# The last three dense graph layers and the norm between them as one stage of 21 blocks

## The reference, cut to what matters

```python
x = x + gated(relu(layernorm(x)))                  # gated layer
x = x + attention(relu(layernorm(x)))              # two attention layers
# from here on: the part that this case is about
h = relu(layernorm(x))
x = x + segment_sum(h[src], dst) / max(deg, 1)     # mean layer
h = relu(layernorm(x))
t = relu(h @ W_self1 + mean_dst(h[src]) @ W_neigh1 + b1)        # first sage layer
x = x + t @ W_self2 + mean_dst(t[src]) @ W_neigh2 + b2          # second sage layer
```

## Time and profile before

| | |
|---|---|
| median of 3 runs | 2992.27 us (2991.39 to 2993.29) |
| the profiled execution | 2988.12 us, its span 2986.0 us |
| from the first matmul of the first dense layer to the end of the span | 2605.6 to 2986.0 us |
| PE busy over the span | 2342.4 us (78%) |
| DVE, ACT, POOL busy over the span | 2250.7, 1007.8, 862.4 us |
| mean granted clock of PE over the span | 0.915 of full speed |

### The profile page before, as it was taken

The page is one execution under the profiler, slowest core; times in us unless marked ns, Lnnn a source line. Parts: engine busy times, 40 slices in busy tenths (PEclk is TensorE's granted clock), DMA queues, the critical chain, the costliest instruction groups (busy, mean ns, idle before and its releaser), DMA issues. The chain is left out here.

```text
span 2986.0 us, 52389 instructions
## 1 busy us (share of the span) xinstructions
PE 2342.4 (78%) x12594; PEld 1568.4 (53%) x12708; DVE 2250.7 (75%) x10890; ACT 1007.8 (34%) x2354; POOL 862.4 (29%) x906
## 2 busy tenths in 40 slices
PE   3676597489999999278867899999964888397868
PEld 1444486245555555156663455555532766275656
DVE  5666666889999999954478899999997444745434
ACT  1777696150100000123365100000011335364434
POOL 0000000017777776100000677777730000000101
PEclk8999799699999999599988999999987999697979
DMA  1000600249999999065532899999943554240121
GB/s 27 1 2 3 289 14 6 67 143 340 339 339 330 330 329 321 0 156 162 156 73 97 272 343 335 326 334 329 332 140 77 164 162 111 69 214 27 35 70 29
DMA packets 403361, 514.58 MB, mean 172 GB/s; under 512 B 31435, under 2 KB 337350, under 8 KB 401542
## 3 DMA queue, kind: packets, MB, share of 16 engines
q1 hardware_dynamic: 335266, 235.04, 27.1%
q0 software_dynamic: 66560, 274.39, 25.4%
q10 hardware_dynamic: 1252, 1.80, 0.2%
HBM read 412.46 MB, written 98.65 MB: 171 GB/s over the span
## 5 line engine op out<-in xcount | busy, mean ns | idle before, releaser
L961 POOL DMA_INDIRECT rows<-row_table,idx x832 | 793.4, 954 | 579.8 <-POOLq L140 302.3
L1012 PE MATMUL z_ps<-xr,hot_ta 128*128 x2400 | 660.5, 382 | 50.0 <-DVE rows L1055 19.4
L1023 PE MATMUL z_ps<-rows,ident 128*128 128x256 f32 x1664 | 567.9, 423 | 7.7 <-DMA rows<-row_table,idx 6.5
L1055 DVE SCALAR_TENSOR_TENSOR rows<-rows,att_all 128x128 f32<-128x128 f32 x1664 | 417.2, 287 | 3.5
L1012 PEld LDWEIGHTS z_ps<-xr,hot_ta 128*128 128x128 bf16 x2496 | 241.2, 97 | 326.0 <-issue 211.2
L1055 DVE SCALAR_TENSOR_TENSOR rows<-z_ps,att_all 128x128 f32<-128x128 f32 x1664 | 406.9, 280 | 0.0
L1398 PE MATMUL acc_m<-xr,hot_m 128*128 x1984 | 341.4, 293 | 76.6 <-issue 52.7
L1398 PEld LDWEIGHTS acc_m<-xr,hot_m 128*128 128x128 f32 x1984 | 282.8, 195 | 141.7 <-issue 136.6
L1081 DVE TENSOR_TENSOR rows<-z_ps,rows 128x256 f32<-128x256 f32 x832 | 346.9, 417 | 8.3 <-PE z_ps L1023 8.3
L1023 PEld LDWEIGHTS z_ps<-rows,ident 128*128 128x128 f32 x1664 | 252.6, 192 | 109.6 <-DMA rows<-row_table,idx 14.8
L2249 PE MATMUL dense_ps<-cnt,h_part 128*128 128x512 f32 (+1 forms) x525 | 218.3, 416 | 106.3 <-ACT cnt L2230 93.5
(11 more groups left out here) (442 smaller groups left out, 3652.0 us busy)
## 6 DMA issues: line engine op xcount, KB each, us to landing
xr<-kept_rows SPq DMA_DIRECT2D x124, 512.0 KB, 4.1
kept_rows<-rows SPq DMA_DIRECT2D x416, 128.0 KB, 5.4
spread_a<-rel_rows SPq DMA_DIRECT2D x208, 128.0 KB, 5.3
counts_line<-counts SPq DMA_DIRECT2D x1, 19550.0 KB
counts<-counts_line SPq DMA_DIRECT2D x6, 3200.0 KB, 18.1
rows<-row_table,idx POOLq DMA_INDIRECT x832, 5.7
row_table<-xl_ring SPq DMA_DIRECT2D x50, 258.0 KB, 2.0
rows<-row_table SPq DMA_DIRECT2D x32, 320.0 KB, 7.6
```

Of the source, the lines that this page charges most:

```text
L961: nc.gpsimd.indirect_dma_start(out=rows[:, u, :], out_offset=None, in_=table, in_offset=bass.IndirectOffsetOnAxis(ap=c.idx[:, n:n + 1], ax ...
L1012: nc.tensor.matmul(ps[:, n % Z, :], hot, tile[:, m, 0:HC], start=m == 0, stop=False, skip_group_check=True)
L1023: nc.tensor.matmul(ps[:, n % Z, HALF_C:HC], c.ident[:, :], rows[:, n % ROWS, HALF_C:HC], start=False, stop=True, skip_group_check=True).th ...
L1055: return nc.vector.scalar_tensor_tensor(out=rows[:, n % ROWS, h * C:(h + 1) * C], in0=z, scalar=0.0, in1=g.att[:, h * C:(h + 1) * C], op0= ...
```

## The change

`dense_layer` and its three calls, the second `norm_relu` and the stage of reloads go. One function, `last_layers`, does all three layers in one stage without a barrier inside: 21 blocks g = 0 to 20, seven in each layer, in the order first big, small, then the other five big ones.

- **Small block.** The counts (56 + 8 + 16 = 80 columns) are the weights, and both parts of h, side by side (256 columns), the moving operand: one matmul in a step, no transposing of the sums afterwards. It took two matmuls of 72 columns.
- **Fix.** A big block's fix follows its own last step (for the first two blocks of a layer, step 8 of the third). The one-hot operand is made by DVE, from uint16 numbers.
- **Results in pieces.** `finish` of a block comes after step 4 of the next, and DVE's element work is cut into five or six pieces, placed at steps 7, 10, 11, 14, 19, 20. PSUM sums have 3 banks.
- **Norm inside.** In layer 0 a block's result goes on at once to its layer norm: statistics on DVE, square root, relu and the high part on ACT, the low part on DVE, all tile by tile at the steps of the next block.
- **Reload.** The new parts of h are stored as they are made, and loaded back group by group (5, 4, 4, 4, 4 tiles) in the layer's last block as soon as its matmuls have used the old ones; the last block's own four tiles are written straight to `parts`. The source tiles are taken in the order 24, 0, 1, ..., 23. DVE casts for odd steps and the last one (13), ACT for 12.
- **Counts.** Their 7 transfers are issued in the `norm_relu` before, and nobody waits for them there. `counts` has one window more; `gated_layer` therefore saves one more window, and its ring is `RINGS = 2`.
- x, h and their space: h stays allocated, its space holds `cnt` and `sum_t`; x is stored to `x_line` block by block, its space then holds weights and results.
- At the very end one more clearing of semaphores and one more barrier.

```diff
@@ norm_relu
-                    sp.wait_ge(s["loads"], 16 * loads(sp, s["loads"]))
+                    if (count := loads(sp, s["loads"])) > 0:
+                        sp.wait_ge(s["loads"], 16 * count)
@@ gated_layer
-        RINGS = 3
+        RINGS = 2
-        high_w = counts[:, SPARE:SPARE + PEAK_WINDOWS, :]
+        high_w = counts[:, SPARE:SPARE + 1 + PEAK_WINDOWS, :]
@@ last_layers (for dense_layer)
+    ORDER = [0, SMALL] + list(range(1, SMALL))
+    BUFS = 4
+    SUMS = 3
+    FIX = 8
+    TILES = [NODE_TILES - 1] + list(range(NODE_TILES - 1))
+    GROUPS = [range(0, T + 1)] + [range(j, j + T) for j in range(T + 1, NODE_TILES - T, T)]
...
+                def add(g, j):
...
+                    if layer(g) > 0 and place(g) == 0:
+                        for b, group in enumerate(GROUPS):
+                            if j == group[0]:
+                                pe.wait_ge(s["loaded"][b], layer(g) * 16 * (4 if b == 0 else 2))
+                        if j == GROUPS[-1][-1] + 1:
+                            pe.wait_ge(s["made"], g)
+                    if small(g):
+                        last = nc.tensor.matmul(
+                            sums(g, 0, 2 * P, slice(0, NARROW)).rearrange("p (k c) -> p k c", k=2),
+                            cnt[:, n % BUFS, 0:NARROW], parts[:, :, k, :], start=j == 0, stop=False,
+                            skip_group_check=True)
+                    else:
+                        last = both(sums(g, 0, BANK), [parts[:, b, k, :] for b in range(2)], cnt[:, n % BUFS, :],
+                                    j == 0, False)
...
+                for g in range(CHUNKS):
+                    for j in range(NODE_TILES):
+                        add(g, j)
+                        if place(g) == 2:
+                            if j == FIX:
+                                fix(g - 2)
+                                fix(g - 1)
+                                if layer(g) > 0:
+                                    turn(g - 2)
+                            if j == 13:
+                                finish(g - 2)
+                            if j == 15 and layer(g) > 0:
+                                turn(g - 1)
+                                turn_own(g - 1)
+                            if j == 22 and layer(g) > 0:
+                                finish(g - 1)
+                        if j == 4 and g > 0 and place(g - 1) in BIG:
+                            finish(g - 1)
+                        if j == 23 and place(g) in BIG and layer(g) > 0:
+                            turn(g)
+                    if place(g) in BIG:
+                        fix(g)
+                finish(CHUNKS - 1)
@@ ACT: after the cast of step j
+                        if g > 0 and place(g - 1) in BIG:
+                            if j == 2:
+                                copy_sums(g - 1)
+                                if layer(g - 1) > 0:
+                                    copy_turned(g - 1)
+                            if layer(g - 1) == 0:
+                                if j == 12:
+                                    normalize(g - 1, 0)      # square root, waits for DVE's piece 2
+                                if j == 15:
+                                    normalize(g - 1, 1)      # relu of two tiles, waits for piece 3
+                                if j == 16:
+                                    normalize(g - 1, 2)      # relu of two tiles
+                                if j == 18:
+                                    normalize(g - 1, 3)      # high part of four tiles
...
@@ DVE: after the cast of step j
+                        if place(g) == 2:
+                            if j == 3:
+                                peak_parts(g - 1)
+                            if j == FIX:
+                                peak_hot(g - 2)
+                                peak_hot(g - 1)
+                            if j == 13 and layer(g) > 0:
+                                own_sum(g - 1)
+                            if layer(g) == 0 and j in (16, 17, 18, 21, 24):
+                                result(g - 2, (16, 17, 18, 21, 24).index(j))
+                            if layer(g) > 0 and j in (16, 17, 18, 20, 22, 24):
+                                result(g - 2, (16, 17, 18, 20, 22, 24).index(j))
+                        if place(g) == 3:
+                            if layer(g) == 0 and j in (1, 3, 4, 6, 9):
+                                result(g - 2, (1, 3, 4, 6, 9).index(j))
+                            if layer(g) > 0 and j < 6:
+                                result(g - 2, j)
+                        if g > 0 and place(g - 1) in BIG:
+                            if j in (7, 10, 11, 14, 19):
+                                result(g - 1, (7, 10, 11, 14, 19).index(j))
+                            if j == 20 and layer(g - 1) > 0:
+                                result(g - 1, 5)
+                    if place(g) in BIG:
+                        peak_hot(g)
@@ SP
+                for n in range(LAYERS_ALL - 1):
+                    first, last = n * PER, n * PER + LAST
+                    for g in range(first, last - 1):
+                        if n == 0:
+                            keep_x(g)
+                        keep_parts(g)
+                    load_parts(last, 0)
+                    if n == 0:
+                        keep_x(last - 1)
+                    for b in range(1, len(GROUPS) - 1):
+                        load_parts(last, b)
+                    keep_parts(last - 1)
+                    load_parts(last, len(GROUPS) - 1)
...
@@ graph_layers
-        dense_layer(nc, c, counts, parts, inv_deg, x, dst, counts_line=counts_line)
...
+        def restore(sp, sem):
+            for k, q in enumerate([0, len(chunks) - 1] + list(range(1, len(chunks) - 1))):
+                low, size = chunks[q]
+                size += 1 + PEAK_WINDOWS if q == len(chunks) - 1 else 0
+                sp.dma_start(counts[:, low:low + size, :], counts_line[:, low:low + size, :]).then_inc(restored[k], 16)
+            return 0
+
+        norm_relu(nc, c, x, h, add=h, loads=restore, parts=(parts[:, 0, :, :], parts[:, 1, :, :]))
+        last_layers(nc, c, counts, parts, inv_deg, x, h_wide, dst, restored,
+                    ((W_self1, W_neigh1, b1), (W_self2, W_neigh2, b2)), h_tables, x_line, out)
+        nc.clear_and_free_semaphores(restored)
+        nc.all_engine_barrier()
```

More of the change, by code:

```diff
@@ L2216, in dense_layer @@
-        with phase(nc, cast_a=0, cast_d=0, cast_p=0, used=0, summed=0, sum_t=0, turned=0, h_t=0, prod=0, vec=0, res=0,
-                   nodes=0, numbers=0, nodes_in=0, peaks=0, peak_c=0, high=0, low=0, zeros=0, loads=0, x_in=2, stored=2,
-                   restored=len(chunks)) as (block, s):
-            def cast(engine, copy, o, k, done):
-                n = step(o, k)
-                q, low, size = chunks[o]
-                size = columns_of(o) // W_NODES
-                if k < 2 and counts_line is not None:
-                    engine.wait_ge(s["restored"][o], 16)
+        own_node = sb("peak_node", [PEAK_COLS, PER])
@@ new lines, in last_layers, with _, cast @@
+        with phase(nc, cast_a=0, cast_d=0, hot=0, used=0, summed=0, turned=0, h_t=0, prod=0, vec=0,
+                   left=0, made=0, nodes_in=0, nodes=0, numbers=0, number=0, peak=0, peak_t=0, zeros=0, loads=0,
+                   x_kept=0, kept=0, loaded=len(GROUPS), x_in=2, stored=2, var=0, std=0, scaled=0, normal=0, high=0,
+                   own_part=0, own_sum=0, own_turned=0) as (block, s):
+            @block.gpsimd
+            def _(pool):
+                nc.gpsimd.iota(columns[:, :], [[1, BANK]], base=0, channel_multiplier=0,
+                               allow_small_or_imprecise_dtypes=True).then_inc(s["numbers"], 1)
+            def cast(engine, copy, g, j, done):
+                n, k = step(g, j), TILES[j]
+                low, size = whole[ORDER[place(g)]]
+                if small(g):
+                    size = NARROW // W_NODES
+                if layer(g) == 0 and j < 2:
+                    engine.wait_ge(restored[place(g)], 16)
@@ new lines, in fix @@
+                def fix(g):
+                    n = fix_step(g)
+                    if place(g) == 0:
+                        pe.wait_ge(s["peak_t"], 2 * layer(g) + 2)
+                    pe.wait_ge(s["hot"], g + 1)
+                    hot = cnt[0:PEAK_COLS, n % BUFS, :]
+                    if small(g):
+                        last = nc.tensor.matmul(
+                            sums(g, 0, 2 * P, slice(0, NARROW)).rearrange("p (k c) -> p k c", k=2),
+                            hot[:, 0:NARROW], peak_t[:, :, :], start=False, stop=True, skip_group_check=True)
+                    else:
+                        last = both(sums(g, 0, BANK), [peak_t[:, b, :] for b in range(2)], hot, False, True)
+                    last.then_inc(s["used"], 1)
@@ new lines, in turn, with turn_own @@
+                def turn(g):
+                    if g > PER:
```

(20 more changed lines are left out.)

598 lines of the change are left out of this document (353 added, 245 removed).

## The result

The changed kernel took 2927.11 us (median of 4 runs, 2922.93 to 2931.8) beside 2992.17 us for the kernel before on the same chip: a ratio of 0.9783, 95% interval 0.9766 to 0.98. Its profiled execution took 2922.93 us, with a span of 2921.1 us and a mean clock of 0.925 (forecast: 2910.8 and 2908.7). From the stage's first matmul to the end of the span it is 321.0 us, where it was 380.4.

A forecast was written before the change was run, and what follows sets the result against it. PE's three gaps before the dense layers, 93.5 us, were taken as the bound. Start 2600.6, layers 95.0, 99.1 and 98.4, tail 10.2 and waits 5.4 gave span 2908.7, profiled 2910.8, plus 4.15: 2915 us; range 2898 to 2941.

The forecast's parts named there:

- Start: Stage's first matmul: counts issued 20 us earlier, so PE starts at 2600.6, 5.0 us earlier; transfers cost the norm nothing.
- Block 0: First wide block of the stage: six steps at half clock, then 19 steps by 0.467, 14.0 us.
- Small block: Block with 80 weight columns and 256 moving: a buffer's round trip sets the pace, 4.2 us; bounds 2.7 and 10.7.
- that rival: Clock falls at the small block: it takes 5.3 us and the next 5 us run at half; 2929 us, chance 10%.
- Sage blocks: Big blocks of the sage layers: stall shrinks to some 0.15 us, so 15.4 us each, 15.3 in the last layer.
- the rival in which the pieces don't fit: Big blocks lose 1.5 us each in sage layers, 1 in layer 0: 23 us, 2938 us, chance 13%.
- Layer 0: Big blocks with the norm inside: 14.6 us each; the third 17.0 and the fourth 16.0.
- the 5.4 us added for waits: Allowance of 0.3 us per big block for waits between engines that the walk along PE doesn't see.
- Boundaries: Between layers: both gaps, 42.9 us, go; a reload group, stored and loaded late in the last block, arrives in time.
- The rival of a late reload: A reload group takes 12 us, not 3.5; PE waits about 8 at each boundary: 21 us, 2936 us, chance 9%.
- Clock: PE's clock rises about 5 us after dense work begins; half clock only for the first six steps.
- Tail: From the end of the last fix to the span's end: 10.2 us instead of 10.6, if finish runs at full clock.

The follow-up runs named there:

- e0: The changed kernel run again, unedited, as the control: 2928.62 us.
- e7: Changed kernel, but SP issues the two peak-node loads in the norm, just ahead of the 7 counts transfers: 2903.09 us.
- e1: Changed kernel, but the peak nodes are loaded in the kernel's first phase instead of by SP in the last stage: 2911.41 us.
- e2: Changed kernel, but ACT's queue issues the two peak-node loads at the stage's start instead of SP's: 2907.54 us.
- e6: e2, but in the sage layers a big block's result pieces run in one go behind step 21, not spread over steps: 2933.47 us.
- e9: e7, but every part of the reload waits for the last step of the layer's last block, not tile by tile: 2915.14 us.
- e3: Changed kernel, but all 7 counts transfers are issued at the start of the last stage, behind the peak nodes: 2926.55 us.
- e5: e2, but POOL again makes the one-hot operand of each fix, instead of DVE: 2907.38 us.
- e8: e7, but in layer 0 block g=2's one-hot goes ahead of its first result, and bn_aggr moves from piece 1 to 2: 2903.79 us.
- e4: Changed kernel, but only three counts transfers are issued in the norm, the last 4 in the last stage behind the nodes: 2909.17 us.

## Why the prediction was right, and where it failed

- **What bounds the kernel.** Right: the three gaps of the earlier trace rows were the first thing to win, and after the change the two between layers have no successor.
- **Start.** 2600.6 forecast, 2600.08 measured, and 2602.75 in e0 with the same kernel, so that the agreement to 0.5 us is in part luck. But "the transfers beside the norm cost it nothing" was followed only for casts and bandwidth, not for SP's queue: the step counted the DMAs that move and not those that are moved past. The nodes' transfer, the same instruction in the same place as before, got 19.5 MB ahead of it.
- **Block 0.** This is the step that failed: 14.0 forecast, 39.2 measured, a 23.49 us wait and a second start at half clock: the mechanism of the queue was missing, not a size. e7 removes exactly this and nothing else, and gives 25.4 us back; e1 and e2 do it in two other ways. With it in place the forecast would have been 12 us too high instead of 12 too low: the span of e7 is 2900.0 with a start 3.8 us later than forecast.
- **Small block.** 4.2 forecast for the 25 matmuls, 4.38 measured, at full clock. The estimate of 2.7 from the Trainium skill (TensorE: Matmul & The Clock Gate, LDWEIGHTS) is not borne out: a weight load of 80 columns shows 147 ns here, where its 67 were taken. Whether it, the casts (258 ns on ACT) or the round trip sets 0.175 a step was not tried. The clock did not fall there, so that rival fails.
- **Sage blocks.** 15.4 and 15.3 forecast, 15.24 and 15.23 measured. The cutting in pieces is what does it, as e6 shows; "the stall shrinks to some 0.15" was right to 0.15, and the rival in which the pieces don't fit falls. The third block of each sage layer was forecast 19.0 and 18.6 and took 18.1 in both, the fourth 15.8 and 15.7 and took 15.3 and 15.4, the first 13.9 and 14.0 and took 13.2 and 13.6.
- **Layer 0.** 14.6 forecast, 14.0 measured; the third and fourth block 17.0 and 16.0 against 16.4 and 14.8 (15.9 in e0, by the clock). The walk added the lateness of DVE and of ACT; most likely one covers the other, which was not tried.
- **The other side of the sum.** Outside the gap PE's waits in the stage sum to 6.0 us (0.6, 2.8, 1.2 and 1.4). The walk itself had named the one at the third block's fix (1.2) and had most of the one in the tail (1.4) in its 10.6 and its 0.5 for ACT's second copy; the other 3.4 are smaller than what it had too much elsewhere, so the 5.4 us added for waits were not needed at all. Without its gap and half clock, layer 0 takes 91.6 us where 95.0 were forecast, the sage layers 96.8 and 97.3 where 99.1 and 98.4 were: 3.4, 2.3 and 1.1 too high. With the 5.4, 0.5 at the start and 0.4 in the tail that is 13.1 us, against the 25.4 of the gap.
- **The prediction's own range.** By its own terms (small block 2.7 or 6 us, waits 0 or 0.9 a block) the sum gives 2905 to 2931 and not 2903 to 2926.
- **Boundaries.** No wait at the steps named. The reload as such was rightly judged near its lower bound: 4.95 us for its first group, with its issue, in e9. The rival of a late reload fails. The Trainium skill's rule for it (DMA: Bandwidth & Descriptors, Measured) changes nothing here: transfers of 256 KB and less moved 223 GB/s in e9's gap, and the time ahead was enough: the first group was issued 11.4 us before the next layer's first matmul (2705.76 to 2717.11), the last 7.0 us before its step 17 (2719.21 to 2726.26).
- **Clock.** The first rise came 4.0 us after the first matmul, 5 forecast; in the other executions of this stage it lies between 2.9 (e9) and 6.1 us (e2). "PEclk at 0.50 anywhere after 2607" was named as a sign of error, and it was one.
- **Tail.** 10.2 forecast from the end of the last fix, 9.8 measured (2911.33 to 2921.1), the finish at full clock, as the sum had taken it; that was luck, as it ran at half clock in e0 with the same kernel (by 1.2 us longer). The extra barrier cannot be seen: from the issue of the output to the end it is 3.7 us in both kernels.

So the median came within 0.4% with two errors of 25 and 13 us of opposite sign in it: the range was met in part by luck. Not one of the rivals had the wait that occurred. The small block's new form and the norm inside the blocks were not taken back by a run of their own; their shares are read from the rows before and after.

## What to carry to other kernels

When a large transfer is moved earlier, write down everything that its queue still has to issue behind it and who waits for that, however small; the small loads go ahead of the large one. A long run of element work is worth cutting up where it holds back the casts that feed PE: it costs its stall, and in e6 the clock after it too. Of a boundary's cost only the last few us (4.4 of waiting and 2 of half clock in e9) came back when the reload waited for the whole block; the rest had gone with the separate stages. And before a difference of 1 to 2 us is put down to an edit, compare the granted clock of the same stretch in both executions.

## What the runs showed of the hardware that was not expected

- Two tiny transfers behind 19.5 MB on SP's queue landed after 29.1 us; on ACT's queue, with the same traffic, after 7.1 us.
- The length of a stall alone did not decide whether PE's clock fell. The wait of about 1.4 us before the last finish (1.36 to 1.39 in all eleven profiled executions of this stage) was followed by 0.50 in seven of them (e0, e1, e2, e3, e5, e6, e8) and by a finish at 1.00 in four (the changed kernel, e4, e7, e9). The wait of 1.2 us at the third block's fix was followed by 3.4 us at 0.50 in e0, e1 and e2, and by none in the changed kernel and in e6. Stalls of 1.92 us lowered the clock in e6 each of four times, one of 1.94 at the third block's fix in e9 did not, nor did 1.57 in the kernel before or 1.00 (e6, last layer). What else decides was not tried.
- A matmul with 80 columns of weights and 256 moving ones ran at a clock of 1.00, which the wide blocks before it had raised, and they follow each other by 0.175 us; the narrow block of before, 51 matmuls of 72 columns in 10.7 us from an idle start, stayed at 0.50.
- The two small loads moved to the first phase (e1) came with attention stages that ended 5 to 12 us later than in the other kernels. The cause is open.
